# A new order of TensorE's work inside a quarter: values and denominators first, then row tile, side piece, row tile

## Time and profile before

| | |
|---|---|
| median of three runs | 2020.81 us |
| the profiled execution's own time | 2023.26 us |
| its span, first to last instruction | 2021.1 us |
| PE busy | 1764.6 us, 87% |
| DVE busy | 1304.5 us, 65% |
| ACT busy | 1063.2 us, 53% |
| GpSimd (POOL) busy | 736.1 us, 36% |
| PE's share of the chain that ended last | 65% (DVE 14%, "issue" 8%) |
| granted TensorE clock, mean of the span | 0.94 |
| the same from 130 to 1390 us | 1.00 |

### The profile page before, as it was taken

The page is one execution under the profiler, slowest core; times in us unless marked ns, Lnnn a source line. Parts: engine busy times, 40 slices in busy tenths (PEclk is TensorE's granted clock), DMA queues, the critical chain, the costliest instruction groups (busy, mean ns, idle before and its releaser), DMA issues.

```text
span 2021.1 us, 39456 instructions
## 1 busy us (share of the span) xinstructions
PE 1764.6 (87%) x12233; PEld 836.5 (41%) x12408; DVE 1304.5 (65%) x3804; ACT 1063.2 (53%) x1898; POOL 736.1 (36%) x759
## 2 busy tenths in 40 slices
PE   3999999999999999999999999999963698999934
PEld 1223343333334343333434343343343577777722
DVE  1665777777677777767777777767555354554435
ACT  1245554656555564655555465655631566666612
POOL 2101112331414233241424234141344577777720
PEclk9799999999999999999999999999975799999955
DMA  2112021221303032130303123030113455433369
GB/s 71 31 33 64 11 64 28 70 68 31 97 12 87 12 87 58 41 97 12 87 12 87 41 57 78 20 87 1 45 35 118 138 153 165 149 111 110 101 188 320
DMA packets 130826, 155.29 MB, mean 77 GB/s; under 512 B 19678, under 2 KB 93170, under 8 KB 130688
## 3 DMA queue, kind: packets, MB, share of 16 engines
q1 hardware_dynamic: 113792, 117.76, 21.3%
q0 software_dynamic: 16896, 35.69, 5.2%
HBM read 65.03 MB, written 55.84 MB: 60 GB/s over the span
## 4 chain that ended last, share of the span: by engine, by line
PE 65%; DVE 14%; issue 8%; SPq 3%; DMA 3%; POOL 3%; ACT 3%; POOLq 0%; another core or an unknown queue 0%; DVEq 0%; ACTq 0%
PE psum L1491 12%; PE psum L1509 10%; PE psum L1548 10%; PE psum L1528 10%; DVE rowmax L1148 8%; PE psum L1597 4%; PE psum L1610 3%; PE psum L1357 3%; POOL y_scratch L658 2%; PE psum L1512 2%; DMA y_scratch<-avn,d_tile 2%; PE psum L1431 2%; PE psum L1410 2%; PE psum L1364 2%; PE psum L1385 2%
## 5 line engine op out<-in xcount | busy, mean ns | idle before, releaser
L1148 DVE TENSOR_REDUCE rowmax<-psum 128x1 f32<-128x512 f32 x1024 | 676.9, 682 | 261.2 <-PE psum L1548 204.0
L757 ACT ACTIVATE probs<-psum 128x1024 f32<-128x1024 f32 x256 | 248.1, 1021 | 263.3 <-PE psum L1512 245.6
L1548 PE MATMUL psum<-arena 128*128 128x512 bf16 x850 | 309.0, 395 | 50.6 <-DVE rowmax L1148 35.0
L757 ACT ACTIVATE arena<-psum 128x1024 f32<-128x1024 f32 x256 | 247.8, 1019 | 174.4 <-PE psum L1512 174.4
L1548 PEld LDWEIGHTS psum<-arena 128*128 128x128 bf16 x1024 | 92.5, 98 | 539.6 <-DVE rowmax L1148 371.5
L585 POOL DMA_INDIRECT sorted_scratch<-rows,slot_idx x256 | 250.3, 978 | 166.8 <-DVE slot_idx L1136 91.8
L1509 PE MATMUL psum<-qk 32*128 32x512 f32 x2048 | 296.1, 648 | 5.1 <-DVE rowmax L1148 3.4
L575 POOL CAST part<-qk 128x512 bf16<-128x512 f32 x64 | 40.2, 628 | 438.5 <-ACT qk L692 438.0
L1597 PE MATMUL psum<-qk 128*128 128x256 f32 x544 | 152.6, 404 | 23.1 <-DVE qk L1281 16.1
L1610 PE MATMUL psum<-probs 128*128 x1088 | 155.7, 287 | 1.2 <-ACT probs L824 0.7
L1610 PEld LDWEIGHTS psum<-probs 128*128 128x128 f32 x1088 | 137.8, 195 | 37.0 <-issue 34.1
(11 more groups left out here) (199 smaller groups left out, 2462.5 us busy)
## 6 DMA issues: line engine op xcount, KB each, us to landing
arena<-part SPq DMA_DIRECT2D x256, 128.0 KB, 2.7
qk<-sorted_scratch SPq DMA_DIRECT2D x136, 144.0 KB
probs<-y_scratch SPq DMA_DIRECT2D x64, 256.0 KB, 4.8
x_in<-in_x_dram SPq DMA_DIRECT2D x16, 512.0 KB, 3.7
x_res<-in_x_dram SPq DMA_DIRECT2D x16, 512.0 KB, 4.4
t_scratch<-t SPq DMA_DIRECT2D x16, 512.0 KB
arena<-t_scratch SPq DMA_DIRECT2D x8, 1024.0 KB
out_dram<-probs SPq DMA_DIRECT2D x32, 256.0 KB, 5.2
```

Source lines behind the costliest of these rows:

```text
L757: a.activation(prob_groups[kb][:, 2 * i:2 * i + 2, :].rearrange("p s n -> p (s n)"), st_pair[i], ACT.Exp, scale=float(C) ** -0.5).then_inc ...
L1148: v.tensor_reduce(rowmax[:, half, kh, h, j:j + 1], row_ps[kh][:, :], AX.X, ALU.max)\
L1548: t_.matmul(row_ps[kh][:, :], qs1[:, par, h, qb * P:(qb + 1) * P], ks1[:, par, h, kh * HALF:(kh + 1) * HALF], start=True, stop=True)\
```

## The change

Each quarter of TensorE is put in one order: values (odd quarters), then the denominators' steps 0 and 1, then scores (even quarters), row tile 0, side piece, row tile 1. The denominators' step 0 leaves `piece` and stands beside step 1, with the same wait for the shared bank in front of it. No instruction is added or removed, and the other engines' programs stay as they are.

```diff
@@ piece
-                elif name[:3] == "den":
-                    free_shared(name, pair, p)
-                    denominators(name, b, 0)
-                    return
@@ iteration
-                    if j % 2 == 0 and in_range(0, pair, p):
-                        b, _, par = image(0, pair, p)
-                        scores(b, par, s, j)
-                    row_tile(0)
                     if j % 2 == 1:
                         lag, sv = (steps_before(s, 1) if j == 1 else (0, s))
                         if in_range(lag, pair, p):
                             b, _, par = image(lag, pair, p)
                             values(b, par, sv, 1 if j == 1 else 0)
-                    if j % 2 == 1:
-                        row_tile(1)
                     for first, lag, half, part_ in DENOMINATORS:
-                        if q == (first + 1) % QUARTERS and in_range(lag, pair, p):
-                            denominators(f"den{half}{'ab'[part_]}", image(lag, pair, p)[0], 1)
+                        for step in (0, 1):
+                            if q == (first + step) % QUARTERS and in_range(lag, pair, p):
+                                name = f"den{half}{'ab'[part_]}"
+                                if step == 0:
+                                    free_shared(name, pair, p)
+                                denominators(name, image(lag, pair, p)[0], step)
+                    if j % 2 == 0 and in_range(0, pair, p):
+                        b, _, par = image(0, pair, p)
+                        scores(b, par, s, j)
+                    row_tile(0)
                     for name in at_quarter(q, pair, p):
-                        piece(name, pair, p)
-                    if j % 2 == 0:
-                        row_tile(1)
+                        if name[:3] != "den":
+                            piece(name, pair, p)
+                    row_tile(1)
```

## The result

The changed kernel takes 2091.97 us (median of four runs, 2091.49 to 2092.96) against 2020.45 us: a ratio of 1.0356, with a 95% interval of 1.034 to 1.0371. It is slower by 71.5 us. The direction was forecast; the size was more than twice the forecast, and the time lies outside the range of 2034 to 2066.

The account below looks back on a forecast made before the run. The prediction took PE as the bound with next to no slack; costs of 5.13 us less gains of 3.00 gave +2.13 us a period, +30 us over 14 periods, so 2051 us on the median, range 2034 to 2066.

Parts of the forecast that it names:

- den0a: Denominator step 0 in q 8: PE waits 0.62 us for DVE to empty the shared bank.
- den0b: Denominator step 0 in q 16: PE waits 0.52 us for ACT to empty the shared bank.
- den1b: Denominator step 0 in q 0, behind usum: PE waits 1.1 us for DVE to empty the shared bank.
- q 27: Both row tiles there wait after DVE's head statistics of q 25: 1.07 and 1.02 us, the largest term.
- zT1: Odd quarter's side piece, now starting before row tile 1: waits 0.37 us for ACT to empty the bank.
- Row tiles 0 of q 25 and 31: With row tiles further apart, their waits for DVE go: gains of 0.75 and 0.51 us.
- Joins: Values and denominators touch in q 1, 9, 17 and 25, saving form changes: net 0.14 us each.
- small pieces: Odd quarters' side pieces start before row tile 1, leaving less time to empty the bank: waits of 0.8 us a period.
- k0: Side piece of an odd quarter: estimated wait of 0.05 us.
- k1: Side piece of an odd quarter: estimated wait of 0.13 us.
- usum: Side piece of an odd quarter: waits 0.22 us for ACT to empty the bank.
- Rival 3: Waits multiply through weight loading, joins saving nothing and late DVE: 4.2 us a period, 2080 us; chance 0.08.

Follow-up runs that it names:

- fill_bank: fill_q26 with the denominator's step 0 back behind scores and row tile 0 in q 0, 8 and 16: 2047.6 us, ratio 1.0138.
- q25_26_old: The changed kernel with the order of before in quarters 25 and 26: 2051.8 us, ratio 1.016.
- odd_join_only: The kernel before, with the new order in q 1, 9 and 17 alone: 2013.0 us, ratio 0.9968.
- fill_kv3: fill_q26 with DVE's last step for the block-diagonal product moved from q 5 to q 2: 2056.88 us, ratio 1.0181.
- fill_q26: The changed kernel with the eight score matmuls of q 26 issued twice: 2062.72 us, ratio 1.0217.
- best_mix_q20: best_mix with the eight score matmuls of q 20 issued twice: 2002.03 us, ratio 0.9909.
- best_mix: The kernel before, with new order in q 1, 9, 17, 21, 23, 29, 31 and step 0 directly behind scores in q 0, 8, 16: 2008.9 us, ratio 0.9942.
- fill_bank_q20: fill_bank with the score matmuls issued twice in q 20 too: 2037.78 us, ratio 1.0086.

## Why the prediction was right and wrong

**Direction and waits: right.** The six larger waits, measured between starts (forecast in brackets), are off by 0.11 us at most: den0a 0.62 (0.62), den0b 0.53 (0.52), den1b 1.10 (1.1), q 27 1.03 and 0.97 (1.07 and 1.02), zT1 0.48 (0.37, from 777.91 to 778.39). fill_bank puts the first three at 2.0 us a period net (by the estimate above), q25_26_old the two of q 27 at 1.0 net.

**The gains: right.** Row tiles 0 of q 25 and 31 no longer wait (the record of the one in q 23 is missing). Joins save what was said: 0.42 us a period for three quarters (odd_join_only), 0.14 x 3 in the sum. In the changed kernel's timeline of q 1, which answers to the earlier trace rows, values and denominators have no gap:

```profile
712.17 1.06 PE L1524 MATMUL psum<-probs,v_sb 128*32 128x512 f32 x8
713.05 1.90 PE L1487 MATMUL psum<-probs,ones 128*32 128x512 f32 x16
714.88 0.61 PE L1544 MATMUL psum<-arena 128*128 128x512 bf16 x2
```

From values to the row tile behind the denominators it is 2.71 us, the 0.86 + 1.85 of the sum.

**The small pieces: mis-sized.** The term was 0.8 us a period. It measured k0 0.14, rank 0.22, k1 0.63, zT1 0.48 and usum 0.32, together 1.8. k1 is the largest miss: the sum took DVE's durations from rows of before, where the product L1049 took 0.58, but the order had moved it under GpSimd's longer instruction, 1.13. fill_kv3 gives this 0.5 us a period. The Trainium skill, SBUF — State Buffer, SBUF: two separate sides, says that VectorE and GpSimd share a pair of ports as an exclusive lock, also for a VectorE instruction with two SBUF inputs, and that the loser waits for the whole instruction. The ends at 726.72 and 726.87 agree roughly: 0.15 us lies between them, where the product takes 0.29 by itself. In the kernel before it was the same with the cast, 0.14 us. With the small pieces as measured the sum is 2.13 + 1.0 = 3.1 us a period where 3.3 was measured; 0.2 stays unassigned.

**The clock: missing.** The sum had every wait at its own length. In the earlier trace rows the clock was 1.00, and I took that as given. This is the step that failed: "a microsecond that PE waits is a microsecond of the period". It is more than one, when the wait is followed by work at 1.2 GHz. 28.7 of the 69.3 us are this, shown by fill_q26, which adds work and is 29 us faster. The other 40.6 are waits net of gains, where the sum had 30; the small pieces, by 1.0 us a period too small in the sum, cover this difference. The two stretches of the kernel before, both behind q 20, stand in periods that are 1.0 and 1.7 us longer than the others (the second of these periods is longer in kernels without a stretch too, 0.9 us in best_mix_q20); they stood in the trace and I didn't ask what they were. Rival 3, waits that multiply, had the nearest time (2080) but not this cause.

The Trainium skill, TensorE: Matmul & The Clock Gate, A second HAM failure mode: psum-queue depth-cycling, describes that frequent short idles between groups of matmuls make the clock fall and rise again. The trace agrees for q 27: in the windows from 788.00 on, PE waited 1.03 and 0.97 us between groups, and the work right behind them ran at 0.52. For q 20, with one wait of 0.4 us ahead of it, the trace can't say whether this or the logits brought the fall.

**Range.** Its upper end, 2066, was built from the unknown prices of operations. The waits with the clock's part nearly out give 2063 (fill_q26), inside it; the clock lies beyond it.

**What stays open.** Why a given period has a stretch behind q 20 and another one not, with the same order of work in both (best_mix has six in the thirteen periods from image 2 on), and why less waiting elsewhere took such stretches away in fill_q26 and brought them in fill_bank. That it can be taken away by filling is shown; which of the two, the wait before the logits or the thin logits themselves, weighs more wasn't tried alone.

## What to carry to other kernels

When PE is the bound and runs at full clock, price a new wait twice: its length, and the chance that work behind it runs at 1.2 GHz, here 1.5 us for a stretch. Look at short windows and not at the mean clock of a stage: 0.96 over a period hid two stretches. How busy PE's records look doesn't tell where the clock will fall, as q 20 shows; the window behind tells it. Where that window runs at 1.2 GHz, useless matmuls that fill the wait can pay for themselves. And before a step is moved ahead on one engine, read what freed its buffer, how late that was, and what other engine's instruction the followers will now meet.

## What was not expected of the hardware

- More work made the kernel faster, three times: 29 us (fill_q26), 10 us (fill_bank_q20), 7 us (best_mix_q20), with 0.86 us of repeated matmuls an image in each.
- Taking waits away can bring stretches at 1.2 GHz: fill_bank lost about 2.0 us of waits a period and got 13 stretches for two.
- A DVE product of 128x128 took 0.29, 0.58 or 1.13 us, by what GpSimd did beside it.
- Filling most of the wait ahead of row tile 0 of q 27 also took away nine of the eleven stretches behind q 20, where nothing was changed (fill_q26).
